# Maxima of causal attention scores in quarters of TensorE, 64 queries at a time

## What is computed

```
scores = einsum('bhqd,bhkd->bhqk', ...) * scale      # layer 0: amplitude/phase features (cos and sin)
scores = where(causal mask, scores, -inf)
attn = softmax(scores, axis=-1)
out = einsum('bhqk,bhkd->bhqd', attn, v) -> (b, s, 128) @ Wo.T
```

## Time and profile before

| | |
|---|---|
| median of 3 runs | 1249.08 us (1247.53 to 1249.44) |
| profiled execution | 1250.84 us, span 1249.3 us |
| mean granted clock of TensorE | 0.892 of full |
| PE (TensorE matmuls) busy | 990.1 us, 79% |
| PEld (weight loads) busy | 647.7 us, 52% |
| DVE (VectorE) busy | 835.6 us, 67% |
| ACT (ScalarE) busy | 680.5 us, 54% |
| POOL (GpSimd) busy | 638.6 us, 51% |

### The profile page before, as it was taken

The page is one execution under the profiler, slowest core; times in us unless marked ns, Lnnn a source line. Parts: engine busy times, 40 slices in busy tenths (PEclk is TensorE's granted clock), DMA queues, the critical chain, the costliest instruction groups (busy, mean ns, idle before and its releaser), DMA issues. The chain is left out here.

```text
span 1249.3 us, 25988 instructions
## 1 busy us (share of the span) xinstructions
PE 990.1 (79%) x8908; PEld 647.7 (52%) x8908; DVE 835.6 (67%) x1829; ACT 680.5 (54%) x1293; POOL 638.6 (51%) x908
## 2 busy tenths in 40 slices
PE   3789753989873999999975463499999599999997
PEld 1456431767662555555533342388888245545553
DVE  1566341799986999999937566033333799999992
ACT  1356443777720777777765353122222377777775
POOL 3467537478764454444533456111110467777775
PEclk9899776899996899999997566699999599999999
DMA  4322032477795222222202233466664112211211
GB/s 136 109 50 53 27 101 85 139 212 204 221 144 124 71 78 73 71 70 70 70 8 57 70 109 103 139 191 183 190 193 139 43 43 53 54 53 54 54 47 32
DMA packets 151526, 122.58 MB, mean 98 GB/s; under 512 B 31712, under 2 KB 134032, under 8 KB 151408
## 3 DMA queue, kind: packets, MB, share of 16 engines
q1 hardware_dynamic: 141664, 102.89, 30.2%
q0 software_dynamic: 8016, 17.71, 5.0%
q10 hardware_dynamic: 1728, 0.46, 0.2%
HBM read 75.75 MB, written 42.61 MB: 95 GB/s over the span
## 5 line engine op out<-in xcount | busy, mean ns | idle before, releaser
L2104 ACT ACTIVATE attend_probs<-attend_attend_ps 128x512 f32<-128x512 f32 x640 | 353.8, 601 | 155.3 <-PE attend_attend_ps L2172 144.2
L2071 POOL TENSOR_SCALAR_AFFINE_SELECT attend_probs<-attend_probs 128x512 f32<-128x512 f32 x256 | 159.7, 636 | 194.1 <-ACT attend_probs L2104 193.4
L2172 PE MATMUL attend_attend_ps<-attend_q,attend_ks 50*128 50x512 f16 (+3 forms) x1024 | 235.8, 306 | 22.9 <-ACT attend_probs L2104 20.3
L2140 PE MATMUL attend_attend_ps<-attend_ks,attend_q 48*128 48x512 f16 (+3 forms) x1024 | 191.1, 316 | 30.5 <-DMA attend_ks<-k_stack 22.9
L2185 PE MATMUL attend_attend_ps<-attend_probs,attend_vals 128*32 128x512 f32 (+3 forms) x2048 | 178.3, 445 | 0.0
L2267 DVE TENSOR_REDUCE attend_neg_max<-attend_attend_ps 128x2 f32<-128x1024 f32 x128 | 155.7, 1216 | 13.4 <-PE attend_attend_ps L2152 12.7
L2152 PE MATMUL attend_attend_ps<-identb,stairs 64*128 64x128 bf16 (+1 forms) x1280 | 144.3, 213 | 0.0
L2172 PEld LDWEIGHTS attend_attend_ps<-attend_q,attend_ks 50*128 50x128 f16 x1024 | 70.4, 94 | 119.3 <-ACT attend_probs L2104 72.6
L2269 DVE TENSOR_REDUCE attend_neg_max<-attend_attend_ps 128x2 f32<-128x768 f32 x128 | 121.9, 953 | 7.7 <-PE attend_attend_ps L2152 6.9
L2152 PEld LDWEIGHTS attend_attend_ps<-identb,stairs 64*128 64x128 bf16 x1280 | 104.0, 100 | 19.5 <-issue 4.7
L1887 PE MATMUL experts_experts_ps<-experts_rowsT,experts_w_in 128*128 128x256 f32 (+1 forms) x468 | 110.6, 387 | 1.6 <-ACT experts_rowsT L1836 1.5
(11 more groups left out here) (317 smaller groups left out, 1990.4 us busy)
## 6 DMA issues: line engine op xcount, KB each, us to landing
experts_w_in<-in_L_ffn_w_dram SPq DMA_DIRECT2D x78, 176.0 KB, 2.4
q_stack<-middle_parts SPq DMA_DIRECT2D x24, 256.0 KB
k_stack<-middle_parts SPq DMA_DIRECT2D x24, 256.0 KB
attend_q<-q_stack SPq DMA_DIRECT2D x64, 96.0 KB
attend_ks<-k_stack SPq DMA_DIRECT2D x64, 96.0 KB
middle_w_in<-in_L_ffn_W_dram SPq DMA_DIRECT2D x23, 256.0 KB
middle_w_out<-in_L_ffn_W_dram SPq DMA_DIRECT2D x23, 256.0 KB
experts_rows<-sorted POOLq DMA_DIRECT2D x39, 128.0 KB, 2.5
```

The costliest lines, as they stand in the source:

```text
L2071: pool.affine_select(out=block_, in_=block_, compare_op=ALU.is_ge, fill=0.0, base=0, pattern=[[0, GH], [1, P]], channel_multiplier=-1).the ...
L2104: act.activation(probs[:, u.par, 2 * c + side, :], ps[:, PROB + side, :], ACT.Exp, scale=SCALE ** -2)\
L2140: pe.matmul(ps[:, bank + side, col:col + (qt + 1) * P], q[rows(side, KR), g, pair, qt * P:(qt + 1) * P], ks[rows(side, KR), g, pair, 0:(qt ...
L2172: mm = pe.matmul(ps[:, PROB + side, col:col + S - kt * P], ks[rows(side, KM), g, pair, kt * P:(kt + 1) * P], q[rows(side, KM), g, pair, kt ...
```

## The change

Maxima are taken in blocks of 64 queries (`QS` = 8 of them) instead of 128, `H` = 64. For each block, pair and side there is one matmul with 64 rows (the side) and 64 output columns (the half that `half(side, pair)` names), so that the four heads of a unit fill the four quarters of the array; the bank now belongs to the pair and its two halves to the sides. A block qs streams (qs + 1) x 64 keys. The five chunks hold the blocks 7; 6 and 0; 5 and 1; 4 and 2; 3. One stair per quarter and chunk is left, of 64 columns a block. Matmuls of scores go from 16 to 32 a unit, stairs stay at 20.

VectorE reduces each block by itself: eight instructions of (pairs x keys) 2 x 512, 2 x 448, 2 x 64, 2 x 384, 2 x 128, 2 x 320, 2 x 192 and 2 x 256 elements, instead of seven.

`max_parts` becomes wider, with zero columns (cleared once in each layer, signal `zeroed`), and the parts are turned by two summed matmuls against an `identh` twice as wide, the second shifted by 64, which swaps the halves for the second pair. The result still is 32 x 128; the two transfers a unit (L2010) now read 32 partitions of 64 queries rather than 16 of 128. The probabilities are computed in two column halves each, so that their tiles fit those of the maxima: 32 matmuls a unit instead of 16, each with the same columns streamed.

```diff
-            pool.tensor_copy(k.identh[:, :], k.ident[:, :]).then_inc(base_set.sem, 1)
+            pool.tensor_copy(k.identh[:, :].rearrange("p (n t) -> p n t", n=2), k.ident[:, :].unsqueeze(1).broadcast_to([P, 2, P]))\
+                .then_inc(base_set.sem, 1)
...
+    H, QS = P // 2, 2 * QT
...
-        neg_max = sb("neg_max", [P, 2, 2, HP, QT])
-        max_parts = sb("max_parts", [P, 2, 2, 2, HP * QT], F16)
-        maxT = sb("maxT", [2 * GH * QT, 2, P], F16)
+        neg_max = sb("neg_max", [P, 2, HP, QS])
+        max_parts = sb("max_parts", [P, 2, HP, 5 * QS], F16)
+        maxT = sb("maxT", [HP * 2 * QS, 2, P], F16)
...
-            if c == 4:
-                return [(0, 1, 0), (1, 1, 256)]
-            return [(c // 2, 3, 0)] if c % 2 == 0 else [(c // 2, 2, 0), (c // 2, 0, 384)]
+            if c == 0:
+                return [(QS - 1, 0)]
+            return [(QS - 1 - c, 0), (c - 1, (QS - c) * H)] if c < 4 else [(3, 0)]
+
+        def half(side, pair):
+            first = H * ((side + pair) % 2)
+            return slice(first, first + H)
...
-                        sp.dma_start(q[64 * side + KR:64 * side + KM, u.group, :, :], maxT[16 * side:16 * side + 16, u.par, :])\
+                        sp.dma_start(q[64 * side + KR:64 * side + KM, u.group, :, :], maxT[:, u.par, H * side:H * (side + 1)])\
...
-                for n, (pair, qt, col) in enumerate(blocks):
+                for n, (qs, col) in enumerate(blocks):
+                    for pair in range(HP):
+                        for side in range(2):
+                            pe.matmul(ps[half(side, pair), bank + pair, col:col + (qs + 1) * H],
+                                      q[rows(side, KR), g, pair, qs * H:(qs + 1) * H], ks[rows(side, KR), g, pair, 0:(qs + 1) * H],
+                                      start=(n == 0), stop=False)
+
+                diagonal = [col // H + qs for qs, col in blocks]
+                apart = diagonal[-1] - diagonal[0] if len(blocks) == 2 else 1
+                for pair in range(HP):
                     for side in range(2):
...
+                        here = slice(64 * side, 64 * side + 64)
+                        span = ps[half(side, pair), bank + pair, :].rearrange("p (n t) -> p n t", t=H)
+                        mm = pe.matmul(span[:, diagonal[0]:diagonal[-1] + 1:apart, :], k.stairs[here, H + H * side:P + H * side],
+                                       k.identb[here, here].unsqueeze(1).broadcast_to([64, len(blocks), H]), start=False, stop=True)
+                    mm.then_inc(scored.sem, 1)
...
+                columns = max_parts[:, u.par, :, :].rearrange("p h s -> p (h s)")
+                for pair in range(HP):
+                    mm = pe.matmul(ps[0:HP * 2 * QS, TURN, 0:P], columns[:, pair * 4 * QS:(pair + 1) * 4 * QS],
+                                   k.identh[:, pair * H:pair * H + P], start=(pair == 0), stop=(pair == HP - 1))
+                mm.then_inc(max_turned.sem, 1)
...
                 for pair, kt, col in prob_chunk(c):
-                    mm = pe.matmul(ps[:, PROB + side, col:col + S - kt * P], ks[rows(side, KM), g, pair, kt * P:(kt + 1) * P],
-                                   q[rows(side, KM), g, pair, kt * P:S], start=True, stop=True)
+                    for first in (0, H):
+                        mm = pe.matmul(ps[first:first + H, PROB + side, col:col + S - kt * P],
+                                       ks[rows(side, KM), g, pair, kt * P + first:kt * P + first + H], q[rows(side, KM), g, pair, kt * P:S],
+                                       start=True, stop=True)
                 mm.then_inc(prob_ps.sem, 1)
...
+            dve.memset(max_parts[:, :, :, :], 0.0).then_inc(zeroed.sem, 1)
...
+                for qs, col in max_chunk(c):
+                    ins = dve.tensor_reduce(neg_max[:, u.par, :, qs], pair_banks[:, :, col:col + (qs + 1) * H], X_AXIS, ALU.max, negate=True)
                 ins.then_inc(maxed.sem, 1)
...
+                if not u.past(1):
+                    dve.wait_ge(zeroed.sem, 1)
```

45 lines of the change are left out of this document (9 added, 36 removed).

## The result

The changed kernel takes 1272.72 us, the median of 4 runs (1269.60 to 1277.89), the kernel before 1249.26 us on the same chip (4 runs, 1247.53 to 1250.39). The ratio is 1.0191, with a 95% interval of 1.0154 to 1.0229: slower by some 23 us, where 1245.0 was forecast with a range up to 1259. The profiled execution of after took 1269.60 us, with a span of 1268.0 against 1249.3. Executions can fall into a slower state; where a kernel ran more than once, the times and ratios in this document are those of its fast runs.

What follows compares the result with a forecast made beforehand. TensorE was taken to bound a step, waiting on ScalarE from c4 to the turning, then matmuls, with VectorE close beside. Terms -2.6, -0.9 and -0.6 us, TensorE's about 0, gave -4.1: 1245.0 us, range 1237 to 1259.

Steps and rivals of the forecast that it cites:

- The step that failed: c3 of `attend1`: its mix starts 0.84 us after it, 0.67 in `attend0`; ScalarE's unexplained 0.22 us got no term.
- rival 2: `attend1`: ScalarE and GpSimd close the loop and absorb VectorE's gain; only -1 us, 1248; chance 0.22.
- rival 1: c3 of `attend1`: ScalarE's lateness goes too, 0.84 and 1.12 us fall to 0.67; 1237.3 us; chance 0.16.
- the sum: All terms of the likeliest case: -4.1 us, TensorE's own about 0 a step; 1245.0 us, chance 0.38.
- More instructions: TensorE, both layers: 53 to 86 loads a unit, mostly covered; +0.05 us a step, bounds 0 and 0.5.
- rival 4: TensorE: the two column halves of one side take turns; +53 us, 1298; chance 0.07.
- Rival 3: c1, c2, c3 and the turn: 25 further loads uncovered for 10 ns each; +0.2 us a step, 1257.4; chance 0.17.
- Columns and the turn: TensorE: c1 and c3 lose 0.055 us each through fewer columns; the two-matmul turn of the maxima adds 0.055 a step.
- The 0.11 us of `attend1`: VectorE's late quotient delays the turned maxima there; shorter reduces remove it in 24 of 32 steps, -2.6 us.
- that saving on TensorE: c4 and c0: fewer columns, 0.03 and 0.19 us shorter, behind the matmul ScalarE waits for; gain nothing.
- The starts of the layers: First two steps of each layer, VectorE's reduces back to back: 0.47 us a step, half taken, -0.9 us for both layers.
- c4's reduce: VectorE, end of a step: falls from 1.23 to 0.68 us, nearly all of the 0.47 us saved per unit.

Runs made afterwards that it cites:

- e9: The kernel before with its matmuls of maxima and probabilities of 256 or more columns split in two along the moving columns; 1268.07 us, one run.
- e13: e9 with layer 1's second gather left out, the first branch added twice; 1244.31 us, one run.
- e1: The changed kernel with layer 1's second gather left out, the first branch added twice; 1243.02 us, one run.
- e7: The changed kernel with layer 1's second gather moved behind the first mask of the step; 1249.26 us, ratio 1.0010.
- e10: The changed kernel with its probability halves of 256 or more columns split in two along the moving columns; 1280.44 us, one run.
- e5: The kernel before with c4's reduce on VectorE covering only half its columns; 1245.55 us, ratio 0.9982.
- e14: The kernel before with layer 1's second gather behind the first mask and the joins right behind that gather; 1242.12 us, ratio 0.9945.
- e15: The changed kernel with layer 1's second gather behind the first mask and the joins right behind that gather; 1247.66 us, ratio 0.9979.
- e3: The changed kernel with probabilities over the full column width again, maxima still in quarters; 1335.3 us, ratio 1.0696.
- e4: The kernel before with only the probabilities computed in two column halves; 1397.11 us, one run.

## Why the prediction was wrong

**The step that failed** is the one on c3 of `attend1`. The prediction read from the earlier trace rows that the second side's exponential comes late there, wrote that what holds ScalarE isn't clear, saw the gather beside it, and then kept that lateness as it was (forecast, rival 2) or let it shrink (rival 1). No case let the step grow by it. It did: the step went to 8.37 us instead of the forecast 7.38, and the 28 steps of `attend1` grew by 20.2 us, where the medians differ by 23.5. An unexplained wait was carried through the sum as a constant, though the change altered one of the two things that the runs show it to hang on: the number of TensorE's instructions beside it (e9, e13); the other is the gather's place (e1, e7). A hole of 0.22 us that the sum cannot explain ought to have been a rival with both signs.

**More instructions** were priced as loads that are covered or not, 0.05 us a step within 0 to 0.5. As TensorE's own work they stayed in these bounds: `attend0`'s 28 steps grew by 1.3 us in the whole, 0.045 a step where the sum had about 0. If the columns gave all that they were priced at, c1 to c3 leave 0.13 us for the instructions. e10 puts 24 further hidden ones at 212.66 - 211.97 = 0.7 us in 28 steps, about 1 ns each, and e9, in full width, at 213.46 - 210.70 = 2.8 us, 4 ns each. The estimate of 1.07 us for the 20 loads of c2, under rival 4, isn't borne out: c2 takes 0.64 us with them. Rival 3 is thus true only in small (0.09 us in the usual step, where it had 0.2), and its place was wrong. Where the loss was, in `attend1`, it had the right sign by another mechanism and not the price.

**Columns and the turn.** In `attend0` after the change:

```profile
502.85 0.63 PE L2208 MATMUL attend_attend_ps<-ident,attend_mixT 128*128 128x128 f32 x4 [0.17 <-ACT attend_mixT L2136]
...
504.08 1.06 PE L2200 MATMUL attend_attend_ps<-attend_probs,attend_vals 128*32 128x512 f32 x8
504.97 0.28 PE L2172 MATMUL attend_attend_ps<-identh,attend_max_parts 128*32 128x128 f16 x2
505.17 0.35 PE L2186 MATMUL attend_attend_ps<-attend_q,attend_ks 50*64 50x384 f16 x2
...
505.81 0.85 PE L2200 MATMUL attend_attend_ps<-attend_probs,attend_vals 128*32 128x384 f32 x8
...
507.18 0.35 PE L2186 MATMUL attend_attend_ps<-attend_q,attend_ks 50*64 50x384 f16 x2
...
507.81 0.86 PE L2200 MATMUL attend_attend_ps<-attend_probs,attend_vals 128*32 128x128 f32 x16
```

The turn to c2 takes 0.20 us (0.16 in the earlier trace rows); as a mean of the layer's usual steps that is +0.05, as forecast. c3 takes 0.63 (0.67), in the mean -0.03, half of the -0.055 forecast. c2, with the same columns, takes 0.64 (0.60), in the mean +0.03, which leaves the bare instructions as the reason. c1 did not get its 0.055: it went from 0.66 to 0.68. From c4 to the turning it is 2.16 instead of 2.13. In sum 7.32 us a usual step instead of the forecast 7.23. Rival 4 is false: the two halves of a side start together (`505.17 0.35 ... x2`).

**The 0.11 us of `attend1`** came as forecast, but under the loss. The turned maxima follow the mix by 0.88 us (1181.50 to 1182.38), where it was 0.99. With one gather in both kernels the changed one gains 1.3 us in 28 steps while it loses 1.3 in `attend0`, so the term is worth -2.6 us, the number of the sum. Its mechanism was only half right: e5 shortened the reduce alone, and the split, caught beside GpSimd's mask and then its joins, ate the gain. In the changed kernel (e1, `attend1`) c4's matmuls are shorter too, so that its reduce starts 5.79 us into the step and not 6.11. The first half of the split is over when the mask starts, the second takes 0.62 us beside it, and both are over before the joins: c0's reduce starts at 0.03 us of the step instead of 0.46. The prediction had priced that saving on TensorE at nothing. So the size of this term came out by a path that the prediction did not have, which is in part luck.

**The rest.** VectorE was to fall to about 22 of 25 us: it is 23.01 in `attend0`, for the split takes 0.62 us there in many steps, and lower only in `attend1`, by waiting. The starts of the layers were to gain 0.9 us and gained nothing (+0.4 and +0.3); TensorE's granted clock was 0.50 in both kernels while `attend0` began (395 to 407), the case in which the prediction expected nothing. c4's reduce takes 0.69 us as a mean (0.68 forecast).

```profile
L2279 DVE TENSOR_REDUCE attend_neg_max<-attend_attend_ps 128x2 f32<-128x512 f32 x27 | 18.7, 693 | 0.0
...
L2293 DVE SCALAR_TENSOR_TENSOR attend_max_parts<-attend_neg_max,attend_max_parts 128x16 f16<-128x16 f32 x27 | 14.0, 520 | 0.9
```

**What stays open.** By what path a gather's preparation holds TensorE's updates, what ends the hold, and why the number of TensorE's instructions matters, no run shows. That it is the update and not the matmul is read from the trace; that the loss grows with the number of matmuls and depends on the gather's place is shown (e1, e7, e9, e13), with single runs for e1, e9 and e13 but 28 steps in each. A kernel with a direct transfer at that place wasn't tried.

## What to carry over

A wait for TensorE isn't proof that TensorE was late: compare the end of the matmuls with the start of what they release, and where a gap remains, look at what GpSimd is issuing beside it. An unexplained wait beside a changed part is not a constant of the sum; it needs a rival in which it grows. Before splitting matmuls, move gathers and joins to where no update of TensorE is awaited; here that alone brought 0.55% (e14), and with the split of the matmuls on top no gain clear of noise (e15).

## What the runs showed of the hardware

- TensorE's semaphore updates were held for up to 1.5 us beside an indirect gather, VectorE's and ScalarE's were not. The hold of c2's second side grew with TensorE's matmuls a unit, 0.53 us at 53, 1.26 at 77 (e9), 1.39 at 86, and hardly further at 110 (e10); the usual step went from 7.50 to 8.25, 8.37 and 8.42. The Trainium skill (TensorE: Matmul & The Clock Gate, The cost: per-tile semaphore tail) says that increments stand in line at 26.3 ns each. In the step above the two held updates of the stairs come 42 ns apart. The change has no more increments a unit than before, and a delay of 1.4 us isn't made of a few of them, so that rule doesn't explain it.
- Tiles of 64 columns in the array did not run beside a tile of 128 columns (e3, e4), only beside tiles of their own width. The usual step was 8.57 us in e3 and 8.87 in e4 at a clock of 1.00, where the two compared kernels have 7.32 and 7.23. The profiles of e3 and e4 also have stretches at 0.50 early in the layers, with steps of 14.3 and 14.6 us, so their whole times (1335.3 and 1397.11 us) say less.
- VectorE's small split instructions from SBUF to SBUF took 0.62 to 0.65 us instead of 0.17 beside GpSimd's mask (e5, after) and 0.33 to 0.39 beside its joins (before, e5); with the joins moved they are back at 0.17 (e14). The Trainium skill (GPSIMD Engine Reference, Specifications) has the two engines share their SBUF interfaces, with contention for VectorE instructions with two SBUF inputs or in a 2-port mode. The trace agrees for the second half of the split, which has two such inputs (0.62 us); the first half has one and took 0.65 beside the mask, and whether it ran in a 2-port mode no trace shows.
- Outside the two attentions, where the code is the same but for one constant, the two profiled executions differed by 9.6 us, and tails of a layer came at a clock of 1.00 in one profile and 0.86 to 0.95 in others: a difference of a few us between single profiles is to be looked for in the steps, not in the span.
